# Gate logits of the first layer from the projection and the values' matmul, and the scatter in the projection's step

## The reference, cut to what matters

```python
out = attention(x) @ Wproj + bproj
x1  = layernorm(x + out)                    # per token, over 128 channels
gate_logits = x1 @ gate_w.T                 # [tokens, 16]
probs = softmax(gate_logits); top1 = argmax(gate_logits)
mask = one_hot(top1); ranks = cumsum(mask) - 1     # place of a token in its expert
mask = mask * (ranks < capacity)                   # capacity 320 tokens per expert
# a kept token goes to slot (expert, rank); its weight is probs[top1]
```

## Time and profile before

| | us |
|---|---|
| median of 3 runs (lowest, highest) | 889.63 (889.05, 891.15) |
| the profiled execution | 898.68 |
| its span on the core | 896.9 |
| mean granted TensorE clock of it, as a share of full speed | 0.952 |
| PE busy | 784.3 (87%) |
| DVE busy | 527.1 (59%) |
| ACT busy | 466.9 (52%) |
| POOL busy | 307.5 (34%) |

### The profile page before, as it was taken

How to read it: one execution, slowest core, us unless ns; L and a number is a source line. 1 busy time by engine, 2 the same in 40 slices (tenths; PEclk the granted TensorE clock), 3 DMA queues, 4 the chain that set the end, 5 groups by cost and what they waited for, 6 DMA issues and landing times.

```text
span 896.9 us, 19631 instructions
## 1 busy us (share of the span) xinstructions
PE 784.3 (87%) x7317; PEld 443.1 (49%) x7317; DVE 527.1 (59%) x1390; ACT 466.9 (52%) x742; POOL 307.5 (34%) x460
## 2 busy tenths in 40 slices
PE   1698999999829999458999999999999999999993
PEld 0244444444316777313555555555555555555441
DVE  4457888888431111154666657766666775554666
ACT  1387898888712122015644445544444555455575
POOL 3122343344346000233433344443434432224405
PEclk9999999999957999768999999999999999999997
DMA  0275333433214554122433345442344443222003
GB/s 27 77 241 143 105 95 104 106 103 98 60 46 110 147 152 122 49 77 54 100 71 72 78 95 101 102 85 70 77 80 96 101 90 80 64 50 59 1 1 94
DMA packets 111706, 78.05 MB, mean 87 GB/s; under 512 B 12272, under 2 KB 103088, under 8 KB 111616
## 3 DMA queue, kind: packets, MB, share of 16 engines
q1 hardware_dynamic: 107984, 71.16, 32.9%
q0 software_dynamic: 3344, 5.56, 2.4%
q10 hardware_dynamic: 288, 0.13, 0.1%
HBM read 37.86 MB, written 13.63 MB: 57 GB/s over the span
## 4 chain that ended last, share of the span: by engine, by line
PE 30%; SPq 13%; DVE 6%; DMA 4%; issue 3%; POOL 1%; ACT 1%; DVEq 0%; POOLq 0%
PE l_ps_v L1260 7%; PE l_ps_c L1233 6%; SPq L115 6%; SPq L113 5%; PE l_ps_d L1246 3%; DMA q_ring<-l_max_rows 2%; PE l_ps_v L1164 2%; DVE l_rden L1761 2%; PE l_by_query L1184 2%; PE l_by_query L1175 1%; PE l_by_key L1333 1%; PE l_by_key L1215 1%; PE l_ps_m L1153 1%; DVE l_neg_max L1749 1%; PE l_ps_m L1333 1%
## 5 line engine op out<-in xcount | busy, mean ns | idle before, releaser
L1749 DVE TENSOR_REDUCE l_neg_max<-l_by_query 128x6 bf16<-128x768 f32 x128 | 122.5, 957 | 136.6 <-PE l_by_query L1188 134.9
L2015 POOL TENSOR_SCALAR_AFFINE_SELECT l_probs<-l_probs 128x512 f32<-128x512 f32 x128 | 88.4, 691 | 198.8 <-ACT l_probs L1485 198.7
L1485 ACT ACTIVATE l_probs<-l_by_key 128x768 f32<-128x768 f32 x128 | 103.7, 810 | 74.9 <-PE l_by_key L1218 70.3
L490 ACT ACTIVATE l_probs<-l_ps_s,minus_bound 128x1024 f32<-128x1024 f32 x128 | 137.2, 1114 | 2.9 <-PE l_ps_s L364 2.8
L1233 PE MATMUL l_ps_c<-l_probs,l_values 128*64 128x256 f32 (+1 forms) x1024 | 113.3, 343 | 0.0
L1233 PEld LDWEIGHTS l_ps_c<-l_probs,l_values 128*64 128x64 f32 x1024 | 62.9, 137 | 39.6 <-issue 21.1
L379 PE MATMUL l_ps_o<-l_probs,l_vpad 128*32 128x256 f32 x1024 | 80.1, 395 | 0.2 <-ACT l_probs L490 0.2
L1164 PE MATMUL l_ps_v<-w_v,l_xT 128*128 128x512 f32 x128 | 72.5, 649 | 0.4 <-ACT l_values L1506 0.2
L1506 ACT ACTIVATE l_values<-l_ps_v 128x512 f32<-128x512 f32 x64 | 38.2, 596 | 61.9 <-PE l_ps_v L1164 59.5
L1260 PE MATMUL l_ps_v<-w_o,l_ctx 128*128 128x128 f32 x512 | 68.4, 289 | 0.0
L1260 PEld LDWEIGHTS l_ps_v<-w_o,l_ctx 128*128 128x128 f32 x512 | 62.3, 198 | 6.4 <-issue 6.2
(11 more groups left out here) (254 smaller groups left out, 1427.5 us busy)
## 6 DMA issues: line engine op xcount, KB each, us to landing
l_rrep<-rden_d SPq DMA_DIRECT2D x32, 512.0 KB
q_ring<-l_parts SPq DMA_DIRECT2D x192, 64.0 KB
k_ring<-l_parts SPq DMA_DIRECT2D x192, 64.0 KB
w_both<-in_L_ffn_w_dram SPq DMA_DIRECT2D x32, 256.0 KB, 3.1
disp_d<-zeros SPq DMA_DIRECT2D x8, 320.0 KB, 4.1
l_xin<-in_L_attn_x_dram SPq DMA_DIRECT2D x16, 128.0 KB, 2.6
l_xr<-in_L_attn_x_dram SPq DMA_DIRECT2D x16, 128.0 KB, 2.5
x_d<-l_x SPq DMA_DIRECT2D x16, 128.0 KB, 2.1
```

The costliest lines, as they stand in the source:

```text
L490: act.activation(probs[c % RING][:, :], ps_s[c % 2][:, :], ACT.Exp, bias=k["minus_bound"][:, :], scale=SCALE).then_inc(probs_sb, 1)
L1485: act.activation(probs[c % P_RING][:, :, 0:N + P], by_key[:, :, 0:N + P], ACT.Exp, scale=SCALE).then_inc(p_sb, 1)
L1749: dve.tensor_reduce(neg_max[:, :, half, :, h].rearrange("p a u -> p u a"), by_query[:, :, 0:3 * P].rearrange("p u (a q) -> p u a q", a=3), ...
L2015: pool.affine_select(out=corners, in_=corners, compare_op=ALU.is_ge, fill=0.0, base=0, pattern=[[0, 4], [1, P]], channel_multiplier=-1).th ...
```

## The change

The layer norm takes the mean and divides by the standard deviation. With gate weights whose columns are centred (the mean over the 128 channels taken off each expert's column), the gate's product of y is the product of y less its mean; so the logits are, but for the positive factor `rstd` of each token, `y @ centred gate`, and y is x plus the projected context plus the bias. The change uses this:

- `constants` makes a second matmul (ones by `gate_T`) and a further VectorE instruction, which centre `gate_T`.
- `w_val` and `w_proj` get 16 more columns (width `VG` = 144): the centred gate, and the projection's weights times the centred gate. The latter and the bias' share (`gate_bias`) are made once in step -2 (a transpose, two matmuls, four ScalarE instructions; one more DMA, `b_col`, is issued by ScalarE at the start).
- The values' matmul L460 thus gives the input's share of the logits of batch b+1; a new VectorE instruction (`of_input`), last in the step, copies it out of `ps_a[1]` into one of four buffers. The projection's matmul L436 gives the other share, and a second new instruction (`all_logits`), right behind y, adds both.
- Gone in each step are the transpose L445, the ScalarE copy L517, the matmul L450 and the small exponential L529. The differences to the maximum are kept for all batches, and after the last step one multiplication by `rstd`, one exponential over 128x512, and what was there before make the weights.
- `gates`, the ranks' matmuls, `ranks`, `routes` and the scatter now belong to batch b-1 in step b, so the steps end at b = 16.
- TensorE's L412 waits in addition for `of_input`, since it overwrites `ps_a[1]`.

```diff
 # TensorE, chunk 0 of step b, ahead of L412
                         pe.wait_ge(xT_sb, b + 3)
                         at_least(pe, v_sb, (b + 1) * V_OUT)
+                        at_least(pe, of_x_set, b + 1)
...
-                    if c == GATES_AT and real(b - 2):
-                        pe.wait_ge(ln_step, (b - 1) * LN + (1 if real(b - 1) else 0))
...
-                            last = pe.transpose(ps_b[:, j * P:(j + 1) * P], x1[p][:, j, :], ident[:, :])
...
-                            last = pe.matmul(ps_b[:, j * E:(j + 1) * E], x1T[:, j * P:(j + 1) * P], k["gate_T"][:, :],
...
-                    if c == CHUNKS - 1 and real(b - 2):
-                        pe.wait_ge(gate_step, (b - 1) * GATE)
+                    if c == CHUNKS - 1 and real(b - 1):
+                        pe.wait_ge(gate_step, b * GATE)
...
 # ScalarE
+            act.dma_start(b_col[:, :], bproj.unsqueeze(1)).then_inc(w_in, 16)
...
-                    if c == GATES_AT and real(b - 2):
...
-                        act.activation(x1T[:, :], ps_b[:, 0:N], ACT.Copy).then_inc(x1T_sb, 1)
...
-                        act.activation(ex[:, (b - 2) * NB:(b - 1) * NB, :], below[:, :, :], ACT.Exp).then_inc(exp_sb, 1)
...
 # VectorE
+            def of_input(b):
+                at_least(dve, gate_step, (b - 3) * GATE)
+                if b == 0:
+                    dve.wait_ge(fold_sb, 4)
+                dve.wait_ge(v_sb, (b + 1) * V_OUT)
+                dve.tensor_tensor(of_x[b % 4][:, :, :], ps_a[1][:, 0:NB * VG].rearrange("p (j c) -> p j c", c=VG)[:, :, C:VG],
+                                  each(gate_bias[:, :]), ALU.add).then_inc(of_x_set, 1)
+
+            def all_logits(b):
+                s = gate.batch(b)
+                dve.wait_ge(of_x_set, b + 1)
+                s.did(dve.tensor_tensor(logits[:, :, :], ps_b[:, 0:NB * VG].rearrange("p (j c) -> p j c", c=VG)[:, :, C:VG],
+                                        of_x[b % 4][:, :, :], ALU.add))
...
 # VectorE, end of step b
-                if real(b - 2) and not real(b):
-                    ranks(b - 2)
-                    routes(b - 2, hb - 1, p)
-
-            unrolled(step, 2, 2)
+                if real(b - 1) and not real(b):
+                    ranks(b - 1)
+                    routes(b - 1, (b - 1) // 2, o)
+                if real(b + 1):
+                    of_input(b + 1)
+
+            unrolled(step, 2, 1)
             weights()
...
 # GpSimd
-                if real(b - 2):
-                    if b == 2:
+                if real(b - 1):
+                    if b == 1:
                         pool.wait_ge(disp_zero, 16 * (SLOTS // (5 * P)))
-                    at_least(pool, rank_step, (b - 1) * RANK)
+                    pool.wait_ge(ln_step, b * LN)
+                    pool.wait_ge(rank_step, b * RANK)
```

More of the change, by code:

```diff
@@ L168, in _ @@
             pe.wait_ge(cut, 1)
-            pe.transpose(gps[:, :], gate_rows[:, :], k["ident"][0:E, 0:E]).then_inc(gate_turned, 1)
+            pe.transpose(gps[:, 0:E], gate_rows[:, :], k["ident"][0:E, 0:E]).then_inc(gate_turned, 1)
+            pe.wait_ge(step, 5)
+            pe.matmul(gps[:, E:2 * E], k["ones"][:, :], k["gate_T"][:, :], start=True, stop=True).then_inc(gate_turned, 1)
         @block.vector
@@ L213, in l0_layer @@
     G2 = NB * H * 2
+    VG = C + E
     def v_first(j):
@@ L225, in l0_layer @@
         w_qkv = sb("w_qkv", [P, 3 * C], FP32)
-        w_val = sb("w_val", [P, C], FP32)
-        w_proj = sb("w_proj", [P, C], FP32)
+        w_val = sb("w_val", [P, VG], FP32)
+        w_proj = sb("w_proj", [P, VG], FP32)
+        b_col = sb("b_col", [P, 1], FP32)
+        gate_bias = sb("gate_bias", [P, E], FP32)
         b_proj = sb("b_proj", [P, C], FP32)
@@ L343, in step @@
                     sp.dma_start(rows(x1_d, b - 1), x1[o][:, :, :]).then_inc(x1_out[o], 16)
-            unrolled(step, 3, 2)
+            unrolled(step, 3, 1)
             for i in two:
@@ L414, in step @@
                         last.then_inc(qk_ps, 1)
+                        if b == -2:
+                            pe.wait_ge(w_in, W_IN)
+                            pe.transpose(ps_b[:, 0:P], w_proj[:, 0:C], ident[:, :]).then_inc(fold_ps, 1)
+                            pe.wait_ge(fold_sb, 2)
+                            pe.matmul(ps_b[:, 0:E], attT[:, 0:P], k["gate_T"][:, :], start=True, stop=True)
+                            pe.matmul(ps_b[:, E:2 * E], attT[:, P:2 * P], k["gate_T"][:, :], start=True, stop=True)\
+                              .then_inc(fold_ps, 1)
                     if c == CONTEXT_AT and real(b - 1):
                         pe.wait_ge(o_out, b)
-                        at_least(pe, rank_step, (b - 3) * RANK + 2)
+                        if b == 1:
+                            pe.wait_ge(fold_sb, 4)
+                        at_least(pe, rank_step, (b - 2) * RANK + 2)
                         for q in range(NB):
@@ L431, in step @@
                     if c == CONTEXT_AT + 2 and real(b - 1):
[L432 to L433 removed]
                         pe.wait_ge(attT_sb, b)
                         for j in range(NB):
[L436 removed]
+                            last = pe.matmul(ps_b[:, j * VG:(j + 1) * VG], attT[:, j * P:(j + 1) * P], w_proj[:, :],
                                              start=True, stop=True)
                         last.then_inc(proj_ps, 1)
[L439 to L452 removed]
                     if c == CHUNKS - 1 and real(b + 1):
@@ L548, in _ @@
             dve.wait_ge(w_qkv_in, 16)
-            dve.tensor_copy(w_val[:, :].rearrange("p (q r w) -> p q r w", q=QUADS, r=2),
+            dve.tensor_copy(w_val[:, 0:C].rearrange("p (q r w) -> p q r w", q=QUADS, r=2),
                             w_qkv[:, 2 * C:3 * C].rearrange("p (r q w) -> p q r w", q=QUADS, r=2)).then_inc(w_val_set, 1)
+            dve.tensor_copy(w_val[:, C:VG], k["gate_T"][:, :]).then_inc(w_val_set, 1)
             before, dump = k["slots_before"], k["dump"]
@@ L635, in weights @@
             def weights():
-                s = Steps(dve, weight_step, 3).batch(0)
-                dve.wait_ge(exp_sb, B)
-                s.did(dve.tensor_reduce(esum[:, :], ex, AX.X, ALU.add))
+                s = Steps(dve, weight_step, 4).batch(0)
+                dve.wait_ge(pow_step, B * POW)
+                s.did(dve.tensor_tensor(below, below, over(rstd[:, :], E), ALU.mult))
+                dve.wait_ge(exp_sb, 1)
+                s.did(dve.tensor_reduce(esum[:, :], below, AX.X, ALU.add))
                 s.wait()
```

97 lines of the change are left out of this document (53 added, 44 removed).

## The result

| | before | after |
|---|---|---|
| median of 4 runs each, us | 890.39 | 903.23 |
| lowest, highest | 889.05, 892.75 | 901.04, 906.07 |
| ratio after/before, 95% interval | | 1.0143 [1.0115, 1.0172] |
| profiled execution (span) | 898.68 (896.9) | 904.07 (902.3) |
| first layer ends (SP's first load of the experts' input is issued) | 264.54 | 276.83 |

The two profiled executions are only 5.4 us apart, the medians 12.8. The first layer alone is 12.29 us longer in the profile; what lies behind it, which the change doesn't touch, happened to take 6.9 us longer in the profile of before. So the 9 us by which before's profile exceeds the median aren't the profiler's, as the prediction had it: in the other traces the stretch behind that point is 621 to 627 us, too.

A forecast was written before the change was run, and what follows sets the result against it. The prediction took the new wait to chain VectorE's whole step to TensorE's projection, 14.38 us a step against 12.86. Terms 1.3 + 2.0 + 15.2 - 1.6 - 5.4 + 3.0 = +14.5 on the median 889.63 gave 904.1 us, range 894 to 914.

The forecast's parts named there:

- start: Constants and first ScalarE instruction: centring work on TensorE and VectorE +0.9, extra DMA issue on ScalarE +0.4; +1.3 us, bounds 0.7 to 2.0.
- up to step 3: x1 of step 2 ends late behind GpSimd's late DMA, so L421 of step 3 comes +2.0 us later, besides the start.
- ten steps without clock falls: Steps 3 to 13: each 14.38 us instead of 12.86 through the new wait; +15.2 us for ten distances.
- falls of the clock in the ten: TensorE's stall ahead of L412 lowers its clock: two falls in twelve steps at 1.5 us each, +3.0; bounds 0 and +18.
- steps 14 and 15, to y: No L412 to delay there; the removed copy and exponential save ScalarE 0.8 us each: -1.6, bounds 0 to -2.4.
- y to the last scatter: End of the layer: y of the last batch to the last scatter takes 6.15 instead of 11.52 us; -5.4, bounds -4 to -6.
- The seam: L412 waits for `of_input` behind x1, making the step one chain through VectorE and TensorE: 14.38 us against 12.86.
- the 6.94: Time in us from L421's start to the end of VectorE's L687, read from one step; first term of the chain.
- The 0.54: End of L687 to end of x1: GpSimd's late L763 no longer late in a longer step, so 5.59 instead of 6.13 us.
- The new instructions: `all_logits` and `of_input` on VectorE: 0.2 us each, not slowed beside GpSimd, as each has one input in PSUM.
- The clock: TensorE idle 1.7 us ahead of L412 in each step, close to a 1.79 us stall followed by the lower clock.
- The faster rival: L412 in each step: `of_input` is done before TensorE needs it; step 12.54 us, -8.9, total 880.7; chance 0.05.

The follow-up runs named there:

- e1: The changed kernel with `of_input` moved from the step's end to between `ranks` and `routes`; 880.40 us on chip B, ratio 0.9929 to the kernel before.
- e3: The kernel before with only one wait added: L412 also waits for VectorE's previous step to end x1; 906.39 us on chip B, ratio 1.0224.
- e7: The changed kernel unaltered, run again on chip C; 902.36 us, ratio 1.0124 to the kernel before.
- e4: The changed kernel with seven unused TensorE transposes filling the stall ahead of the projection from step 2 on; 897.60 us on chip B, ratio 1.0128 to before.
- e8: e4's kernel (changed kernel, stall filled with seven transposes) again, on chip C beside e7; 898.48 us, ratio 1.0075 to the kernel before.
- e9: e1's kernel again (changed kernel, `of_input` between `ranks` and `routes`), on chip D; 889.71 us, ratio 0.9974 to the kernel before.
- e11: e9's kernel with the gate's centring last among the constants and the bias column loaded by SP; 890.70 us on chip D, ratio 0.9978 to before.
- e12: e1's kernel with GpSimd's scatters held until ScalarE has copied `attT`; 881.27 us on chip E, ratio 0.9944 to the kernel before.

## Why the prediction was right

Forecast 904.1, measured 903.23; range and sign held. The mechanism is shown by e1 and e3: the new wait is late in every step from 2 to 13 (twelve times, 21.5 us in all), e3 loses as much by it alone, and without it the loss is gone. By its steps, from the first layer of the two profiles:

| step | predicted | measured |
|---|---|---|
| start | +1.3 | +1.34 (ScalarE's table load at 13.88 against 12.54) |
| up to step 3, start included | +3.3 | +3.8 (85.12 - 81.32) |
| ten steps without clock falls | +15.2 | +12.5 (10 x 14.11 - 128.62) |
| falls of the clock in the ten | +3.0 (two in the twelve steps) | +3.2 (two; a third, in step 2, is in the row up to step 3) |
| steps 14 and 15, to y | -1.6 | -2.2 (17.28 at y, 19.52 at step 13's L439) |
| y to the last scatter | -5.4 | -5.0 (6.51 against 11.52) |
| sum | +14.5 | +12.3 (last scatter 271.43 against 259.16) |

**The seam.** The chain's five terms, from the time line of 129.14 to 143.25: L439 to the end of L711 6.98 (predicted 7.14 with the sum of the logits), to x1's end 5.52 (5.59), `of_input` another 0.11 (0.2), TensorE's start 0.14 (0.06), L421 to L439 1.36 (1.39). Sum 14.11 against 14.38. Each term was near, and ten times the 0.27 makes 2.7 us: this is the term of the sum that was mis-sized most. The others missed by +0.5, +0.2, -0.6 and +0.4, which nearly cancel. The total fits still better than that, 903.2 for 904.1, partly by luck: before's median rose from 889.63 to 890.39 with its fourth run, and the medians differ by 12.8 where the layers' ends differ by 12.3. Of the 0.16 in the first term 0.10 is the gap of L513: the row that the 6.94 was read from is step 5; in the steps without the gap it is 6.84. The 0.54 that the prediction gave back for GpSimd's late start is borne out by the second term.

**The new instructions.** `of_input` took 187 ns in the mean, the sum of the logits 181, like the row of L611. In after GpSimd had no instruction beside them in 14 of 16 steps, so this says little on contention. In e1 `of_input` lay beside GpSimd's L790 or L779 in all 16 steps and took 191 to 193 ns. There the trace agrees with the Trainium skill ("SBUF — State Buffer", "Who interferes with whom"), by which a VectorE instruction with one input in SBUF, outside the two-port modes, doesn't contend with GpSimd.

**The clock.** The stall was 1.67 to 1.68 us in steps 4 to 13, predicted 1.7; in steps 2 and 3 it was 2.78 and 1.96 (2.68 and 2.15 in e7). Of the ten short ones two were followed by the half clock, in after as in e7, and of the four longer ones three. So after had three falls in the twelve steps, e7 four, at 1.5 to 1.7 us each; the prediction took two at 1.5. e4 and e8 show that the stall is their cause. Its length alone doesn't place them: the eight stalls without a fall are as long as the two with one, and e9 has a stall of 2.63 us at 78.08 without one, before one of 1.79 with.

**The faster rival.** It stood at 880.7, or -8.9, for the case that the wait isn't late. e1 is that case, with steps of 12.47 where it said 12.54, and its layer ends 8.67 us before that of the trace of before (255.87 against 264.54). But on e1's chip before itself had 886.33, so the gain there was 5.9; no trace of before was taken on that chip, so which of its stages is the quicker one isn't shown. By parts the layer gained -3.7 in the ten steps, -3.3 from there to y and -5.0 from y to the last scatter, and lost 3.4 up to step 3. The rival's -0.32 a step looks borne out by -0.37, but 0.30 of that is the gap in before's trace, so this agreement is luck. On chip D the gain was 1.9, with the gap of L524.

**Two points came out, but not for the reasons given.** The start's +1.3 stands in the trace of after, but by e11 it needn't reach the end: the wait for the rings' DMAs in step 1 can absorb it. And the sum was put on the median of the runs although the profile of before was 9 us above it for a reason of its own, behind the first layer; medians and the layer's end agree within 0.6 us (12.84 and 12.29), so nothing was lost by it.

## What to carry to other kernels

Before a wait is added, find the instruction that fulfils it in the other engine's order, and compare its end with the start of the waiter in the time line: here 107.5 against 105.75 told the sign, and the sum around the new chain gave the size to 0.3 us a step. A buffer that the next step overwrites should be read at the earliest place in the reader's order, not at its end: the same 0.19 us instruction moved ahead of the routes turned +1.4% into a gain of 0.3 to 0.7%. Read a step more than once before taking it as the base: before's steps are 12.56 to 13.26, and the longer ones hold the gap ahead of one ScalarE copy, which the change had no part in. And work removed from engines that don't bound a chain is idle time: the change removed TensorE and ScalarE work in every step and the steps grew.

## What the runs showed that was not expected

- The same kernel beside the same kernel before: 0.9929 [0.9901, 0.9958] on one chip and 0.9974 [0.9954, 0.9995] on another, for a 1.0 to 1.2 us gap ahead of one ScalarE copy in each step. A gain of 0.7% on one chip is thus not a property of the kernel alone. The best candidates are e1's kernel and e12's; e12's 0.9944 [0.9923, 0.9965] was had on a chip of the quicker kind, and whether it removes the gap on the others wasn't tried.
- A TensorE stall of 1.67 us, repeated in ten steps, was followed by the lower clock twice in each of two traces; shortened to 0.67, never.
- A VectorE instruction with both inputs in SBUF (the keys' scaling) lasts up to 1.03 us instead of 0.49 where GpSimd's addition of the bias runs beside it, and the step grows by the difference. It sets apart the longer steps of e4, e8 and e9 from the shorter ones.
- The wait alone in the kernel before cost 20.1 us, more than the whole change (12.8). The difference of 7 isn't simply what the removals are worth, since the two were measured on different chips; in the traces, with three falls of the clock each, after's layer ends 4.3 us before e3's (276.83 against 281.17), and the end of the layer, where the last scatter follows y by 6.51 us instead of 11.52, gives 5.0.
